# Which states' input products GpSimd makes, and in which steps VectorE makes the others, in a selective-scan kernel

## The reference

```python
dt = jax.nn.softplus(jnp.einsum('blr,er->ble', dt, dt_proj_w) + dt_proj_b)
A = -jnp.exp(A_log)
def step(h, inp):
    dt_t, B_t, C_t, x_t = inp
    dA = jnp.exp(dt_t[:, :, None] * A)
    h = dA * h + (dt_t * x_t)[:, :, None] * B_t[:, None, :]
    y = jnp.einsum('bds,bs->bd', h, C_t)
    return (h, y)
```

## Time and profile before

| | us |
|---|---|
| median of 3 runs | 16611.66 |
| lowest, highest | 16605.69, 16624.14 |
| the profiled execution, its own time | 16605.28 |
| its span | 16603.5 |

### The profile page before, as it was taken

How to read it: one execution, slowest core, us unless ns; L and a number is a source line. 1 busy time by engine, 2 the same in 40 slices (tenths; PEclk the granted TensorE clock), 3 DMA queues, 4 the chain that set the end, 5 groups by cost and what they waited for, 6 DMA issues and landing times. The chain is left out here.

```text
span 16603.5 us, 158027 instructions
## 1 busy us (share of the span) xinstructions
PE 14390.7 (87%) x30720; PEld 5782.7 (35%) x30720; DVE 15104.1 (91%) x13023; ACT 11266.2 (68%) x18635; POOL 15002.7 (90%) x6275
## 2 busy tenths in 40 slices
PE   6888888888888888888888888888888888888888
PEld 2333333333333333333333333333333333333333
DVE  6999999999999999999999999999999999998988
ACT  5666667666666666666677666667666676667675
POOL 5999889998899989998899998999989999899998
PEclk9999999999999999999999999999999999999999
DMA  3444444444444444444444444444444444444443
GB/s 132 155 154 161 150 152 154 155 157 150 154 154 153 163 145 153 156 154 159 142 155 160 152 160 143 156 156 158 155 143 156 156 157 158 146 148 158 150 151 135
DMA packets 738975, 2535.44 MB, mean 153 GB/s; under 512 B 77240, under 2 KB 78016, under 8 KB 721728
## 3 DMA queue, kind: packets, MB, share of 16 engines
q1 hardware_dynamic: 738112, 2527.45, 44.8%
HBM read 2376.15 MB, written 150.99 MB: 152 GB/s over the span
## 5 line engine op out<-in xcount | busy, mean ns | idle before, releaser
L1467 POOL TENSOR_TENSOR RING<-RING,CS 128x1024 f32<-128x1024 f32 x4096 | 9833.9, 2416 | 1369.6 <-DVE RING L1148 1350.2
L1148 DVE TENSOR_TENSOR_SCAN RING<-DA,HS,RING 128x512 f32<-128x512 f32 x8192 | 9955.4, 1264 | 811.0 <-ACT DA L777 614.1
L388 PE MATMUL YP<-RING,EYE 128*128 128x512 f32 x16384 | 8293.4, 638 | 1648.6 <-POOL RING L1467 1578.7
L777 ACT ACTIVATE DA<-ITEM,AN 128x512 f32<-128x512 f32 x8192 | 5519.4, 685 | 3384.9 <-DVE RING L1148 3376.5
L388 PEld LDWEIGHTS YP<-RING,EYE 128*128 128x128 f32 x16384 | 3133.4, 199 | 6324.9 <-issue 3616.5
L1128 DVE TENSOR_TENSOR RING<-DTP,BS 128x1024 f32<-128x1024 f32 x2816 | 3375.5, 1206 | 0.4 <-DMA BS<-bc_rows 0.3
L1454 POOL TENSOR_TENSOR RING<-ITEM,BS 128x1024 f32<-128x1024 f32 x1280 | 3016.6, 2357 | 9.4
L388 PE MATMUL FL<-XN,WC 128*128 128x512 f32 x4096 | 1943.3, 618 | 9.7 <-ACT XN L864 4.6
L388 PEld LDWEIGHTS FL<-XN,WC 128*128 128x128 f32 x4096 | 839.4, 205 | 1129.8 <-issue 1121.5
L791 ACT ACTIVATE ITEM<-FL,COL 128x512 f32<-128x512 f32 x512 | 347.6, 679 | 1183.1 <-PE FL L388 1183.1
L388 PE MATMUL FL<-LS,WP 128*128 128x512 f32 x2048 | 995.6, 610 | 35.3 <-DVE XR L1184 29.2
(11 more groups left out here) (123 smaller groups left out, 10636.4 us busy)
## 6 DMA issues: line engine op xcount, KB each, us to landing
BS<-bc_rows SPq DMA_DIRECT2D x2048, 512.0 KB, 4.9
CS<-bc_rows SPq DMA_DIRECT2D x2048, 512.0 KB, 3.6
XR<-in_x SPq DMA_DIRECT2D x128, 1024.0 KB, 7.3
x_slices<-XR SPq DMA_DIRECT2D x64, 1024.0 KB, 8.1
XR<-x_slices SPq DMA_DIRECT2D x64, 1024.0 KB, 7.5
out<-XR SPq DMA_DIRECT2D x64, 1024.0 KB, 8.2
XR<-in_wqkv SPq DMA_DIRECT2D x24, 1024.0 KB, 7.3
bc_rows<-ROWS SPq DMA_DIRECT2D x256, 64.0 KB, 4.6
```

The lines of the kernel that those rows point to most:

```text
L388: return pe.matmul(*a, **k)
L777: act.activation(DA[:, h, :], DT[:, i % 2, h, :], ACT.Exp, scale=AN[:, h, s:s + 1]).then_inc(dA_ready, 1)
L1148: dve.tensor_tensor_scan(H[:, slot(n), h, :], DA[:, h, :], U[:, slot(n), h, :], HS[:, i % ITEMS, h, s:s + 1], ALU.mult, ALU.add).then_inc( ...
L1467: pool.tensor_tensor(G[:, slot(n)], H[:, slot(n)], CS[:, s % C_ROWS, :].unsqueeze(1).broadcast_to([P, NH, T]), ALU.mult).then_inc(g_ready, 1)
```

## The change

GpSimd's five states per item are 1, 4, 7, 8 and 10 where they were 0, 1, 2, 7 and 8. With `U_LEAD = 3` it makes them ahead of output products 14 (for the next item), 1, 4, 5 and 7, where it was 13, 14 and 15 (for the next item), 4 and 5. VectorE makes the other eleven in steps 0 (u0), 2 (u2, u3), 4 (u5, u6), 9 (u9), 10 (u11, u12), 11, 12 and 13 (one each); it was steps 2 (u3), 3 (u4, u5), 4 (u6), 7, 8, 9, 10, 11, 12 and 13 (one each, from u9 on). The table of the late windows: u2 in step 2, u3 in 3, u5 in 4, u6 in 5, u11 in 10, u12 and u13 in 11.

```diff
-POOL_U = (0, 1, 2, 7, 8)
+POOL_U = (1, 4, 7, 8, 10)
 NP_U = len(POOL_U)
 ND_U = NS - NP_U
 U_LEAD = 3
-AHEAD = ((), (), (3,), (4, 5), (6,), (), (), (9,), (10,), (11,), (12,), (13,), (14,), (15,), (), ())
-AHEAD_LATE = ((), (), (3,), (4,), (5, 6), (), (), (9,), (10,), (11,), (12,), (13,), (14,), (15,), (), ())
+AHEAD = ((0,), (), (2, 3,), (), (5, 6,), (), (), (), (), (9,), (11, 12,), (13,), (14,), (15,), (), ())
+AHEAD_LATE = ((0,), (), (2,), (3,), (5,), (6,), (), (), (), (9,), (11,), (12, 13,), (14,), (15,), (), ())
```

## The result

| | median, us | runs | lowest, highest |
|---|---|---|---|
| before | 16620.93 | 5 | 16605.69, 16624.83 |
| after | 16702.42 | 5 | 16692.91, 16704.68 |

The ratio is 1.005, with an interval of 1.0036 to 1.0065: 0.5% slower, where 2.4% faster was forecast. The profiled execution after has a span of 16700.6 us, 97.1 more than before.

A forecast was written before the change was run, and what follows sets the result against it. It took a loop of GpSimd's burst, TensorE's sums and the gate as the bound; 21 x 7.6 + 14 x 5.8 + 7 x 9 + 21 x 5 = 409 us off gave 16205 us, range 16020 to 16490.

The forecast's parts named there:

- What bounds the kernel now: GpSimd's burst, TensorE's sums and the gate loop: no window under 59.6 us; 56.5 after, so it ceases to bind.
- Shared port: VectorE's polynomial beside GpSimd's work: kept at 2.0 to 2.4 us; at worst 64 x 1.2 = 75 us more.
- The new longest path of a tile: GpSimd carries window types (w modulo 4) 0 to 2, VectorE type 3: 243.3 us per ordinary tile, 7.6 less.
- At nothing: ScalarE in steps 5 to 9: VectorE waits 0.9 us (types 0, 1) or 1.9 (type 2), off the path.
- Rival (b): ScalarE binds: steps 5 to 9 cost VectorE 2.6 us per window and VectorE carries the tile; 16430 us, 17%.
- The dt product stopping scan 14: GpSimd's later dt product delays a decay factor: VectorE waits 3.9 us in type 1, 2.2 in type 2.
- rival (c): Slower: the later dt product stops scan 14 in every window, 4.6 us each; 17125 us, 9%.
- The 21 long intervals: Tiles of 256 to 277 us, three about the end of each image but the last: 5 us less each.
- the sum: Total of savings: 409 us off the profiled 16605.3, so 16196; with the runs' median 6 us above, 16205.

The follow-up runs named there:

- the two kernels without the port: The kernels after and before, each with the polynomial's second operand from PSUM and a comparison for its product: 16275.56 us and 16268.68 us.

## Why the prediction was wrong

- **What bounds the kernel now: right.** The burst of GpSimd, TensorE's sums and the gate were a loop, and the change broke it: gate 45.7 us where under 200 was the mark, types 3 and 0 shorter by 2.8 and 3.3 us. But GpSimd's waits for scans, which were to fall to about 1000 us, rose to 1426.8.
- **"Shared port": this step failed.** It kept the polynomial at 2.0 to 2.4 us and let at most 75 us be added, 1.2 per tile. In type 1 it took 7.8 us in 42 of 64 tiles and 4.6 to 7.3 in 21, where 2.4 had been usual: 260 us more in that type, 4 per tile. The kernels with GpSimd stepping aside in type 1 and with the polynomial later there gave back 265 and 260 us, and the operand in PSUM 427. The row itself, had a 6.2 us case that the count of one operation did not explain; it was noted and left. The Trainium skill, "SBUF — State Buffer", section "SBUF: two separate sides", has whichever starts first hold the port pair for its whole instruction, with the other blocked. By that the polynomial would wait for one operation of GpSimd (2.35) and take its own 1.2, an estimate of at most 3.55 us; the 7.80 us over three operations of GpSimd is more, and the measurement decides. The port costs before, too, more than its durations show (337 us for 235).
- **"The new longest path of a tile": this step failed with it.** It had GpSimd carry types 0 to 2, trailing by up to 5 us, and asked only what that does to scans and the dt product. That trail is the very state in which GpSimd shuts the polynomial out, and VectorE then carried the tile: what came off its polynomial in type 1 came off the time. 243.3 us per tile was nearly reached (245 to 247) only with the port, the turn's pause and half of the own-product waits gone.
- **"At nothing", ScalarE: on a premise that failed,** that GpSimd carries the tile. Steps 5 to 9 were given 0.9 us per window in types 0 and 1 and 1.9 in type 2; they took 1.3, 1.4 and 2.3, and 4.8 in type 3, where it had been 2.5. Summed over the run by step, the factor wait at scan 8, the last of four steps without a product (three when late), went from 20 to 315 us (65 to 90 in each type), more than the whole rise of 275. With VectorE carrying the tile such waits can count, and in VectorE's ledger of the two kernels without the port they are half of what ate the gain. No run takes them away alone, so what they cost in time is not shown. Rival (b) had this mechanism and its condition; but it had no term for the port either, so its 16430 was missed as well.
- **The dt product stopping scan 14: it did not come in this kernel.** The factor waits at scan 14 are 117 us before and after, 3 us of them in type 1, where 3.9 per window had been put. With the polynomial short they do come there: 91 us with GpSimd stepping aside in type 1, 109 with the operand in PSUM, 1.4 and 1.7 per window. As a limit (rival (c)'s mechanism) the dt product came in the kernels where GpSimd steps aside in every window.
- **Two terms were absent.** A product right ahead of its own scan costs the scan 0.28 us, 525 times, 159.1 us: VectorE's new tables put u0, u9 and, in late windows, u2 and u3 there. No run shortens that wait alone, so its part of the time is not shown. And the packet at the turn of the loop, which was read as nothing of the change, since no DMA was added: but every load is timed by GpSimd's output products, and these moved. It costs 135 us by the kernel with the loads moved.
- **The 21 long intervals** did get shorter, by 3.5 us in the mean (267.5 to 264.0) where 5 were taken.
- **Two slips of the sum** change nothing: 16196 and 6 are 16202, not 16205, and rival (c)'s 256 x 4.6 is 1178, not 1183.

What stays open: what decides that a waiting VectorE operation is passed over once more by a GpSimd that comes from an unbroken run though its next operation is not yet released (182 times, against 99 times let in). No run varied the distance alone. How the 337 us that the port costs the kernel before divide between VectorE's 235 and GpSimd's 224 was not taken apart, nor what the factor waits and the waits for own products cost in time.

## What to carry to other kernels

When a change lets one engine trail another with work in hand, price again every operation that shares a port with it: a wait that was 2.4 us beside an engine that idles can be 7.8 beside one that doesn't. Here moving that operation, taking its operand from PSUM or having the other engine wait for it in that one window gave it back, in whole or in part. Ask also what the removed waits may have covered (short waits for factors, a product right ahead of its scan), and where a moved product now times loads through a semaphore. Put a cure that adds a wait to an engine only in the windows where the stall is: in one window of four it gained the kernel after 265 us, in all four it cost the kernel before 275 (the kernel after was not run with all four alone).

## What the runs showed of the hardware

- A VectorE operation with two SBUF inputs can be passed over by GpSimd's operations several times in a row: 7.80 us for 1.2 us of work. Where GpSimd's next operation was already released, it was passed over until GpSimd ran dry in 271 of 273 cases; where GpSimd had just waited and its next was not released, in none of 822. With the second operand in PSUM all 255 took about 1.19 us.
- GpSimd loses by the port as well: the product behind a polynomial took 3.33 us for 2.35, and its output products took 9833.9 us together with the port shared, 9609.8 without.
- At the 40 back jumps of its loops VectorE stood with no releaser, 4.72 us with the 16 DMA engines 96.8% full of row loads and an instruction packet among them; the sum over the run fell from 161.1 to 38.0 us on VectorE and from 198.2 to 2.6 on ScalarE when the loads came a product later.
- A scan that needs the VectorE instruction just ahead of it waits for it, 0.28 us in the median of 525 cases (159.1 us in all).
